# Cross attention in a decoder layer: reciprocals of the softmax sums in SBUF, row maxima moved by DMA, weighted values in the middle of a unit, both halves of the probabilities added by POOL

## The reference

```
scale = HEAD_DIM ** (-0.5)
scores = einsum('bhtd,bhsd->bhts', q, k) * scale
scores = where(causal_mask, neg_inf, scores)
scores = where(key_padding_mask, neg_inf, scores)
attn = softmax(scores, axis=-1)
out = einsum('bhts,bhsd->bhtd', attn, v)
```

## Time and profile before

| | |
|---|---|
| median of 3 runs | 3406.66 us |
| profiled execution, its own time | 3420.66 us |
| its span | 3418.9 us |
| PE / PEld busy | 3061.5 us (90%) / 1750.2 us (51%) |
| DVE / ACT / POOL busy | 2181.1 (64%) / 1672.3 (49%) / 1718.2 us (50%) |
| mean granted clock of PE | 0.925 of full speed |

### The profile page before, as it was taken

One profiled execution on the slowest core, in us unless ns is written; L12 is line 12 of the kernel. 1 busy time (PEld: TensorE's weight loads), 2 busy tenths in 40 slices (PEclk: granted clock), 3 DMA queues, 4 the chain that ended last, 5 costly groups with the idle time before them and its releaser, 6 DMA issues. The chain is left out here.

```text
span 3418.9 us, 41782 instructions
## 1 busy us (share of the span) xinstructions
PE 3061.5 (90%) x15214; PEld 1750.2 (51%) x15214; DVE 2181.1 (64%) x3987; ACT 1672.3 (49%) x3029; POOL 1718.2 (50%) x694
## 2 busy tenths in 40 slices
PE   7997999999999999999999997696489986989488
PEld 6875444444444444444444442575345542777433
DVE  4334788788888888888888882463265574566322
ACT  2221466666666666666666665221076672222111
POOL 0001388787888878788888878000210001333255
PEclk9998799999999999999999999798696796999679
DMA  4545545646456464465554443597632232333621
GB/s 173 182 174 171 114 93 107 135 94 151 86 109 135 104 143 99 102 133 108 129 113 96 90 93 65 184 265 169 178 113 86 83 94 106 123 123 116 215 72 35
DMA packets 171357, 424.22 MB, mean 124 GB/s; under 512 B 19105, under 2 KB 40514, under 8 KB 151172
## 3 DMA queue, kind: packets, MB, share of 16 engines
q1 hardware_dynamic: 147038, 276.97, 27.9%
q0 software_dynamic: 24128, 144.75, 20.1%
HBM read 170.20 MB, written 124.58 MB: 86 GB/s over the span
## 5 line engine op out<-in xcount | busy, mean ns | idle before, releaser
L654 DVE TENSOR_REDUCE part_max<-ps_s 128x1 f32<-128x512 f32 x2048 | 1270.3, 679 | 313.2 <-PE ps_s L555 313.2
L751 ACT ACTIVATE probs<-ps_st 128x512 f32<-128x512 f32 x2048 | 1086.4, 600 | 549.3 <-PE ps_st L574 533.9
L513 POOL TENSOR_TENSOR added<-added,probs 128x2048 f32<-128x2048 f32 x256 | 1181.9, 4617 | 93.0 <-ACT probs L751 66.9
L555 PE MATMUL ps_s<-k_stack,q_stack 96*128 96x512 f32 x2048 | 842.1, 427 | 28.3 <-POOL max_parts L503 20.6
L574 PE MATMUL ps_st<-q_stack,k_stack 98*128 98x512 f32 x2048 | 857.7, 424 | 6.6 <-ACT probs L751 5.4
L574 PEld LDWEIGHTS ps_st<-q_stack,k_stack 98*128 98x128 f32 x2048 | 386.9, 190 | 505.6 <-ACT probs L751 362.1
L585 PE MATMUL ps_pv<-probs,v_sb 128*32 128x512 f32 x4096 | 547.2, 606 | 0.0
L555 PEld LDWEIGHTS ps_s<-k_stack,q_stack 96*128 96x128 f32 x2048 | 396.0, 193 | 213.9 <-DVE part_max L654 142.8
L521 POOL DMA_DIRECT2D probs<-probs x128 | 112.7, 880 | 232.7 <-PE ps_pv L585 219.1
L1404 DVE TENSOR_REDUCE xneg_max<-xps_s 128x2 f32<-128x308 f32 x256 | 110.6, 448 | 130.8 <-PE xps_s L1325 82.2
L1654 POOL MEMSET e_bias_rows<- 128x1024 f32 x1 | 1.0, 952 | 354.3 <-POOLq L46 354.3
(11 more groups left out here) (268 smaller groups left out, 3633.1 us busy)
## 6 DMA issues: line engine op xcount, KB each, us to landing
probs<-probs POOLq DMA_DIRECT2D x128, 1024.0 KB, 7.0
xq_stack<-q_parts SPq DMA_DIRECT2D x64, 384.0 KB, 4.4
q_stack<-q_hi SPq DMA_DIRECT2D x64, 256.0 KB, 6.1
k_stack<-k_hi SPq DMA_DIRECT2D x64, 256.0 KB, 9.0
q_parts<-q_h_out SPq DMA_DIRECT2D x64, 256.0 KB, 4.9
x_in<-in_x_rows SPq DMA_DIRECT2D x8, 1024.0 KB, 7.1
q_hi<-qk_h_out SPq DMA_DIRECT2D x8, 1024.0 KB, 4.3
q_lo<-qk_l_out SPq DMA_DIRECT2D x8, 1024.0 KB, 6.3
```

The costliest lines, as they stand in the source:

```text
L513: pool.tensor_tensor(added[:, w % 2], left, probs[:, k % RING], ALU.add).then_inc(added_up, 1)
L555: pe.matmul(ps_s[:, place % BANKS], q_stack[0:ROWS, w % 4, j, t * P:(t + 1) * P], k_stack[0:ROWS, w // BPB, j, n * BLK:(n + 1) * BLK], sta ...
L654: dve.tensor_reduce(part_max[:, s:s + 1], ps_s[:, (w * SLOTS + s) % BANKS], AX.X, ALU.max)\
L751: act.activation(probs[:, k % RING, j], ps_st[:, n % BANKS], ACT.Exp, scale=SCALE).then_inc(item_used, 1)
```

## The change

- **Values and totals.** `weighted_values(u-1)` moves to step 4 (`BEFORE_VALUES`), `totals(u-1)` behind step 7. The turn moves to step 2.
- **Addition by POOL.** POOL adds the two halves of the probabilities of each unit into `added`; totals take four matmuls from it instead of eight. POOL starts when the last exponential of the unit and the totals of the unit before are done. The splitting of the weights follows these additions in units 1, 3, ... 11.
- **Sums in SBUF.** ACT copies `ps_d` to `sums` (`sums_out`). DVE takes the reciprocals there, in two pieces of 256 columns, and `normalize` multiplies `sums` by `attn_raw`, both in SBUF. `totals` now waits for that copy, not for `normalized`.
- **Turned rows by DMA.** `max_parts` has 8 columns a tile instead of 128, ACT copies all rows of the turn to `row_parts` at once, and SP moves them to the extra rows of the query tile with four DMAs (`rows_into_place`), which transposed scores wait for.
- **Loads.** Keys for transposed scores and the masks of the exponentials have semaphores of their own, and the second batch's keys and the weights ahead are issued after the second row move.
- **The high part of the maxima** is taken by a tensor_reduce over one element instead of a copy.

```diff
-        BEFORE_TURN = 3
+        BEFORE_TURN = 2
+        BEFORE_VALUES = 4
+        PIECES = 2
...
+        added = sb("xadded", [KH, HEADS, BLK])
-        max_parts = sb("xmax_parts", [P, TPB, P], F32R)
+        max_parts = sb("xmax_parts", [P, TPB, 2 * HEADS], F32R)
+        row_parts = sb("xrow_parts", [2 * HEADS, 2, BLK], F32R)
+        sums = sb("xsums", [P, 2, BLK])
...
@@ SP
+                def rows_into_place(u):
+                    sp.wait_ge(item_used, turn_item(u) + 1)
+                    for j in range(HEADS):
+                        sp.dma_start(q_stack[ROWS:TOP, u % BUFS, j].bitcast(F32),
+                                     row_parts[2 * j:2 * j + 2, u % 2].bitcast(F32)).then_inc(rows_loaded[u % 2], 16)
+                rows_into_place(0)
                 sp.dma_start(v_sb[:], xv_rows).then_inc(v_loaded, 16)
                 load_q(2)
                 load_q(3)
-                load_k(1)
-                ahead.load(sp)
-                for u in range(UNITS + 2):
+                for u in range(UNITS + 3):
+                    if exists(u + 1):
+                        rows_into_place(u + 1)
+                    if u == 0:
+                        load_scores_k(1)
+                        load_transposed_k(1)
+                        ahead.load(sp)
+                    if exists(u - 3):
...
@@ POOL
-                for step in range(ahead.STEPS):
-                    ahead.split_step(pool, step)
+                for u in range(UNITS):
+                    pool.wait_ge(item_used, item(u, TILES - 1) + 1)
+                    if u:
+                        pool.wait_ge(dens_done, u)
+                    pool.tensor_tensor(added[:], probs[:, u % 2, 0], probs[:, u % 2, 1], ALU.add).then_inc(added_up, 1)
+                    if u % 2 and u < 2 * ahead.STEPS:
+                        ahead.split_step(pool, u // 2)
@@ PE
                 def totals(u):
                     if u:
-                        pe.wait_ge(normalized, u)
-                    for h in range(2):
-                        for j in range(HEADS):
-                            mm = pe.matmul(ps_d[j * HD:(j + 1) * HD], ones[:], probs[:, u % 2, h, j],
-                                           start=(h == 0), stop=(h == 1))
+                        pe.wait_ge(sums_done, u)
+                    pe.wait_ge(added_up, u + 1)
+                    for j in range(HEADS):
+                        mm = pe.matmul(ps_d[j * HD:(j + 1) * HD], ones[:], added[:, j], start=True, stop=True)
                     mm.then_inc(dens_done, 1)
...
@@ DVE
-                    dve.tensor_copy(parts[:, :, :, 0], neg_max[:, u % 2]).then_inc(max_high, 1)
+                    dve.tensor_reduce(parts[:, :, :, 0], neg_max[:, u % 2].unsqueeze(3), AX.X, ALU.max).then_inc(max_high, 1)
...
-                    dve.reciprocal(ps_d[:, cols], ps_d[:, cols]).then_inc(inverted, 1)
+                    dve.reciprocal(sums[:, u % 2, cols], sums[:, u % 2, cols]).then_inc(inverted, 1)
...
-                    dve.tensor_tensor(attn_out[:, u % 2], ps_d[:], attn_raw[:, u % 2], ALU.mult).then_inc(normalized, 1)
+                    dve.tensor_tensor(attn_out[:, u % 2], sums[:, u % 2], attn_raw[:, u % 2], ALU.mult).then_inc(normalized, 1)
...
                 for u in range(UNITS + 2):
                     for s in range(SLOTS):
+                        if s == BEFORE_VALUES and exists(u - 2):
+                            invert(u - 2, 0)
                         if exists(u + 2):
                             slot_max(u + 2, s)
-                        if exists(u - 2) and s < 2:
-                            invert(u - 2, s + 2)
-                        if exists(u - 2) and s == 2:
-                            normalize(u - 2)
-                        if exists(u - 1) and 3 <= s < 5:
-                            invert(u - 1, s - 3)
                     if exists(u + 2):
                         max_rows(u + 2)
+                    if exists(u - 2):
+                        invert(u - 2, 1)
+                        normalize(u - 2)
@@ ACT
-                    for j in range(HEADS):
-                        mm = act.activation(q_stack[ROWS:TOP, u % BUFS, j], ps_st[j * HD:j * HD + 2, n % BANKS], ACT.Copy)
-                    mm.then_inc(item_used, 1)
+                    if u >= 2:
+                        act.wait_ge(rows_loaded[u % 2], 64 * (u // 2))
+                    act.activation(row_parts[:, u % 2], ps_st[0:2 * HEADS, n % BANKS], ACT.Copy).then_inc(item_used, 1)
...
+                def sums_out(u):
+                    if u >= 2:
+                        act.wait_ge(normalized, u - 1)
+                    act.wait_ge(dens_done, u + 1)
+                    act.activation(sums[:, u % 2], ps_d[:], ACT.Copy).then_inc(sums_done, 1)
```

More of the change, by code:

```diff
@@ L1225, in cross_attention @@
                                            for n, (_, high, _) in enumerate(weights_ahead)])
-        k_loaded = [sem(f"xk_loaded{b}") for b in range(B)]
+        ks_loaded, kt_loaded = ([sem(f"x{n}_loaded{b}") for b in range(B)] for n in ("ks", "kt"))
         v_loaded = sem("xv_loaded")
         q_loaded = [sem(f"xq_loaded{s}") for s in range(BUFS)]
-        consts_loaded, ones_set, ident_ready = sem("xconsts_loaded"), sem("xones_set"), sem("xident_ready")
+        consts_loaded, masks_loaded = sem("xconsts_loaded"), sem("xmasks_loaded")
+        ones_set, ident_ready = sem("xones_set"), sem("xident_ready")
         scores_done, max_done = sem("xscores_done"), sem("xmax_done")
@@ L1232, in cross_attention @@
         item_done, item_used = sem("xitem_done"), sem("xitem_used")
-        pv_done, dens_done = sem("xpv_done"), sem("xdens_done")
-        raw_done, inverted, normalized = sem("xraw_done"), sem("xinverted"), sem("xnormalized")
+        rows_loaded = [sem(f"xrows_loaded{s}") for s in range(2)]
+        pv_done, dens_done, added_up = sem("xpv_done"), sem("xdens_done"), sem("xadded_up")
+        raw_done, sums_done = sem("xraw_done"), sem("xsums_done")
+        inverted, normalized = sem("xinverted"), sem("xnormalized")
         out_stored = [sem(f"xout_stored{s}") for s in range(2)]
@@ L1337, in turn_max @@
                     for t in range(TPB):
-                        mm = pe.matmul(ps_st[:, n % BANKS, t * P:(t + 1) * P], max_parts[:, t], ident_r[:],
+                        mm = pe.matmul(ps_st[0:2 * HEADS, n % BANKS, t * P:(t + 1) * P], max_parts[:, t], ident_r[:],
                                        start=True, stop=True)
@@ L1345, in transposed_scores @@
                     if t == 0:
-                        pe.wait_ge(item_used, turn_item(u) + 1)
+                        pe.wait_ge(rows_loaded[u % 2], 64 * (u // 2 + 1))
+                        pe.wait_ge(kt_loaded[batch(u)], 16)
+                        pe.wait_ge(masks_loaded, 32)
                     if n >= BANKS:
@@ L1388, in _ @@
                     for t in range(TILES):
-                        if t == BEFORE_TURN:
-                            if exists(u + 1):
-                                turn_max(u + 1)
-                            if exists(u - 1):
-                                weighted_values(u - 1)
-                                totals(u - 1)
+                        if t == BEFORE_TURN and exists(u + 1):
+                            turn_max(u + 1)
+                        if t == BEFORE_VALUES and exists(u - 1):
+                            weighted_values(u - 1)
                         if exists(u):
@@ L1398, in _ @@
                             scores(u + 2, t)
+                    if exists(u - 1):
+                        totals(u - 1)
             @block.vector
@@ L1476, in raw_out @@
                     act.activation(attn_raw[:, u % 2], ps_pv[:], ACT.Copy).then_inc(raw_done, 1)
-                act.wait_ge(ones_set, 6)
-                act.wait_ge(consts_loaded, 80)
+                def sums_out(u):
[3 more added lines that the diff above has]
+                    act.activation(sums[:, u % 2], ps_d[:], ACT.Copy).then_inc(sums_done, 1)
                 max_rows(0)
+                act.wait_ge(masks_loaded, 32)
                 for u in range(UNITS + 1):
                     for t in range(TILES):
-                        if t == BEFORE_TURN:
-                            if exists(u + 1):
-                                max_rows(u + 1)
-                            if exists(u - 1):
-                                raw_out(u - 1)
+                        if t == BEFORE_TURN and exists(u + 1):
+                            max_rows(u + 1)
+                        if t == BEFORE_VALUES and exists(u - 1):
+                            raw_out(u - 1)
                         if exists(u):
                             exponentials(u, t)
+                    if exists(u - 1):
+                        sums_out(u - 1)
 def shared_feed_forward(nc, x1_rows, attn_t, w_h, w_l, w3_h, w3_l, bo, b12, b3, gamma, beta, eye,
```

47 lines of the change are left out of this document (25 added, 22 removed).

## The result

The changed kernel takes 3516.91 us (median of four runs, 3514.61 to 3520.07). The kernel before, its three runs of above and one more, has a median of 3426.44 us. The ratio is 1.0275, with a 95% interval of 1.022 to 1.033: slower by more than 2%. The profiled execution took 3520.07 us, its span 3517.2 us, 98.3 us more than the span before; the mean granted clock fell from 0.925 to 0.889.

What follows compares the result with a forecast made beforehand. PE bound at half clock; at full clock the loop totals, reciprocals, normalization, totals. Terms summed to +99 us, taken as +95: 3515.7 us for the profiled execution, 3502 us as median (before: 3406.66), range 3418 to 3548.

Steps and rivals of the forecast that it cites:

- start and units 0 to 3: Start +2 us (bounds -6 and +8) from reordered loads; units 0 to 3 +8, first additions blocking the max rows.
- 20 plain units: Units without causal mask, 14.9 us each at half clock: 298 against 115.5 + 100.1, +82 us.
- units 14 to 19: Masks add matmuls: about 16.4 us for two units, 12 to 18 for the other four, +10 us.
- last two units: No maxima stand behind the held normalization there, -3 us.
- The wait: DVE's normalization, now with two SBUF inputs, arrives 0.8 us late at half clock and waits until POOL's 4.58 us addition ends.
- The ring: Normalization, maximum, scores, values, steps, totals, POOL's addition: 14.9 us a unit at half clock, 11.2 at full clock.
- PE: Totals go from eight matmuls to four, saving 1.8 us; PE's own work at half clock becomes 12.4 us a unit.
- DVE: Two reciprocals of 256 columns from SBUF take 3.4 us, as four did before; 1.7 was the lower bound.
- rival 4: A reciprocal in SBUF is also held by POOL, 1.7 us in each of 20 units, +34, about 3540 us; chance 0.06.
- SP: Four row moves by DMA a unit, 4.3 us with ACT's copy, are hidden behind 9.8 us at half clock.
- rival 2: DVE reaches normalization before POOL starts, no hold; units 12.4 us at half clock, about 8.3 at full; 3349 us; chance 0.16.
- Clock: PE stops over 3 us a unit at full clock, so the clock falls; plain units run nearly all at half clock.

Runs made afterwards that it cites:

- experiment 1: The changed kernel with the normalization reading the values' PSUM bank instead of their SBUF copy (output not the layer's): 3415.68 us, ratio to before 1.0017.
- experiment 2: The changed kernel with both reciprocals ahead of DVE's slot 4 and the normalization behind slot 5, before POOL's addition starts: 3444.71 us, ratio 1.0062.
- experiment 3: The changed kernel with POOL adding only two of four heads, ones in place of the other sums: 3454.97 us, ratio 1.0098.
- experiment 5: The changed kernel without POOL's addition, totals again by eight matmuls from both halves: 3411.91 us, ratio 0.9987.
- experiment 6: Experiment 2 with the max rows' subtraction written as three reductions of one SBUF input each: 3380.88 us, ratio 0.9873.
- experiment 4: The changed kernel with the row moves by DMA undone, four ACT copies and 128 columns a turn again: 3522.97 us, ratio 1.0287.
- Experiment 7: Experiment 6 with third unit's queries before the first row move, second-batch keys and weights loaded singly in units 2 to 9, splits later: 3325.01 us, ratio 0.9714.
- experiment 9: The changed kernel with only the filler added (one more matmul, identity with zeros, per transposed score tile of units without causal mask): 3541.48 us, ratio 1.0341.
- experiments 1 and 5 to 8: Its 8 is experiment 7 plus the filler, one more matmul of an identity with zeros per transposed score tile of unmasked units: 3317.36 us, ratio 0.9695.
- experiment 11: Experiment 7 with weight splits in odd units 11 to 21 and the filler (extra matmuls with zeros) in plain units 9 to 15 alone: 3330.11 us, ratio 0.9738.
- experiments 8 and 12: Its 12 is the kernel before with only the filler added (extra matmuls with zeros in unmasked units): 3369.66 us, ratio 0.9853.

## Why the prediction was right, step by step

**Size.** The sum was +99, taken as +95, for the profiled execution; the span grew by 98.3. As medians 3502 stood against 3516.91; the executions of the kernel before, from which it was taken off, differ by 50 us among themselves. The terms, from the starts of the first exponentials:

| term | predicted | measured |
|---|---|---|
| start and units 0 to 3 | +2 and +8 | -6.4 (first exponential) and +14.0 = +7.6 |
| 20 plain units | +82 | 151.46 + 151.39 - 115.5 - 100.1 = +87.3 |
| units 14 to 19 | +10 | +7.6 |
| last two units | -3 | -6.1 |
| end and rest | 0 | +1.9 |

**The wait** was the right step. Normalization was to be held until POOL's add ends, and experiments 1, 2, 3 and 5 took the hold away in four ways (another place of an input, another order, a shorter addition, none), each with the half-clock unit that the theory gives. Normalization was to come 0.8 us after the addition's start and came 0.70 after it. The ring was 14.9 us and is 15.13. From the timeline: addition to the end of normalization 5.08 (predicted 4.58 + 0.67), to the released slot 0.44 and to values 0.64 (0.4 + 0.5), values 3.58 (3.57), four steps 3.28 (3.16), totals to the next addition 2.11 (1.8 and handoffs of 0.25). The small excess sits in the first step behind values and in the handoffs. The Trainium skill ("SBUF — State Buffer", "Terms") says that DVE and GpSimd arbitrate for a shared pair of ports, exclusively and for a whole instruction; experiment 3 agrees, since the hold shrank with the addition, to a mean of 2.29 us for an addition of 2.36.

**PE** at half clock was to be 12.4 us of own work; where nothing is held, it is 12.45 (experiments 1, 2 and 6). Totals saved 14.15 - 12.45 = 1.70 us, predicted 1.8. **DVE**: reciprocals were to take 3.4 and took 2 x 1.74 = 3.48, not the lower bound of 1.7. They aren't held (none of the 64 took over 1.75 us), so rival 4 falls. **SP**: the row moves are hidden, as experiment 4 shows, although four issues take 2.41 us and not 4 x 0.34: SBUF to SBUF, 0.60 each. Without holds the full-clock unit is 8.19, where rival 2 had 8.3.

**Start.** Net it came out near the forecast (+7.6 for +10), but of other parts than I summed, and so by luck. The first exponential came 6.4 us earlier, at my lower bound. Units 0 and 1 took 16.68 and 18.87 us in place of 9.50 and 10.69, +15.4 and past my upper bound of 8. The issues of the changed kernel show why; the rows of L1447 and L1368 are the one max row that an addition held:

```profile
2465.26 2.55 SPq L1297 DMA_DIRECT2D xq_stack<-xrow_parts  x4
...
2468.32 2.10 SPq L1270 DMA_DIRECT2D xq_stack<-q_parts  x4
2477.93 0.47 PE L1355 MATMUL xps_s<-xks_stack,xq_stack 96*128 96x154 f32 x1 [7.83 <-issue]
...
2487.16 4.21 DVE L1447 TENSOR_TENSOR xmax_parts<-xneg_max,xmax_parts 128x16 fp32r<-128x16 f32 x1
...
2489.90 3.44 SPq L1270 DMA_DIRECT2D xq_stack<-q_parts  x2
...
2491.43 0.40 PE L1368 MATMUL xps_st<-xident_r,xmax_parts 128*8 128x128 f32 x4 [3.42 <-DVE xmax_parts L1447]
```

The queries of units 2 and 3 were issued only behind the first row move, at 2468.3, and PE stood 7.83 us before the first scores of unit 2 (the row names no releaser; that it was the queries is inferred from the order). Those of unit 4 went out at 2489.9 behind the keys and weights that were moved past them. I had counted what the loads cost the row moves, and not what the row moves cost the query loads. My +8 was for first additions that block the max rows: one did, in unit 1, and PE stood 3.42 us for it, but the hold seems not to have set the unit, for in experiment 6, where no max row is held, unit 1 took 18.61 us all the same, with PE standing 8.12 us for the row moves behind the loads. In return unit 2 was 9.0 us and not 17.87, since the first weight split moved out of it; that gain was missing in my sum. Unit 3 took 16.89 us and not 9.44: PE stood 2.96 us behind the held normalization, and the clock fell. Experiment 7 gets 19.5 us of units 0 to 2 back by the order of loads and splits alone.

**Clock.** Nearly all at half clock was right: 0.50 in both plain groups. The ring of 11.2 us at full clock was never seen in a plain unit. The argument that PE's stop in the ring takes the clock down is borne out: in the changed kernel it fell at 2519.8, at the end of the stop of 2.96 us in unit 3, in experiment 9 the same units with more matmuls lose it behind a stop of 2.44 us, and experiments 1 and 5 to 8, with the ring open, keep it for longer. The stop can't be the only cause, though: in experiment 1 the clock fell at 2742.6 with no wait of PE over 0.58 us, and in the kernel before at 2588.9 with no single wait over 0.85. I had also written that the plain units did not bring the clock back; experiment 11 shows that with the filler they do. What in a plain unit's matmuls decides between the two isn't settled: the filler adds a full-height operand, work and bf16 at once, and I did not separate them. The Trainium skill's rule ("TensorE: Matmul & The Clock Gate", "What's actually happening"), that activity releases the clock, agrees with experiments 8 and 12, and not with the 151 us of the first plain group, where PE counts as busy for 128 us at 0.50, nor with the eight units of experiment 1 where it is busy throughout.

**What I left out.** The max rows' subtraction has two SBUF inputs too. In the changed kernel it is mostly out of POOL's way (mean 0.32 us, once 4.2); as soon as the normalization moves, it takes its place. Of the change's 101 us that experiment 1 gives back, 20 x (15.13 - 12.45) = 54 us are the hold itself in plain units, and some 17 the clock there, which in experiment 1 stood at 1.00 in units 4 and 20 to 22. Some 30 lie in units 3 and 14 to 19, hold and clock together; no run takes these apart.

## What to carry to other kernels

Before work goes to POOL, list the DVE instructions with two SBUF inputs that can meet it: each lasts until the POOL instruction that it meets has ended, whatever its own size, and what is queued behind it on DVE pays too. Leave one input in PSUM, place it ahead of POOL's start, or write it as reductions with one input; not every instruction with one SBUF input is safe, for the cast of the earlier trace rows was held too, 1.36 us against 0.18 in other units. When a step puts a wait on PE, read the granted clock beside every gain: here PE's own work in a plain unit takes 12.45 us at half clock and 8.2 at full clock, a larger difference than the 2.7 us of the hold.

## What the runs showed of the hardware beyond that

- With the next POOL instruction right behind the first, the hold can end with the first: the normalization was through 0.55 us after its end in the changed kernel and in experiment 7. It then delays that next one: POOL's cast of 128 x 1024 took 1.49 us there, against 1.03 us in experiment 1, and the addition behind the split in experiment 7 took 4.99 us against a mean of 4.58. But the hold can also last through both: two normalizations of experiment 9 took 7.99 and 7.96 us, an addition and the split behind it, and three of experiment 3 likewise. What decides between the two isn't settled. The first of experiment 9:

```profile
2526.68 4.53 POOL L1337 TENSOR_TENSOR xadded<-xprobs 77x2048 f32<-77x2048 f32 x1 [10.34 <-PE xps_d L1405]
...
2528.23 7.99 DVE L1460 TENSOR_TENSOR xattn_out<-xsums,xattn_raw 128x512 f32<-128x512 f32 x1
...
2531.18 4.49 POOL L74 TENSOR_TENSOR xwo_w_l<-xahead_raw,xwo_w_h 128x2048 fp32r<-128x2048 f32 x1
```

- Eight matmuls with zeros a unit cost a plain unit 0.2 to 0.4 us at full clock, made the kernel before 1.5% faster (0.9773 to 0.9933) and reduced the spread of its runs from 62 to 7 us.
